# Quantised feed-forward constants set up by DMA and spread over two batches, with x's statistics first, in a fused cross-attention and feed-forward kernel

## The reference, cut to what matters

```
qh = softmax(Wq @ layernorm(x), over the 64 of a head) * 64**-0.5
kh = softmax(Wk @ c, over tokens);  vh = Wv @ c
out = Wo @ ((kh vh^T)^T qh) + bo
x = x + out / |out| * g * sqrt(128)            # |out| over the channels
w = (nibbles(qweight) - round(zeros / scales)) * scales      # 1024 x 1024
x = x + layernorm(x) @ w + bias
```

## Time and profile before

| | us |
|---|---|
| median of 3 runs (lowest, highest) | 718.89 (718.29, 720.46) |
| the profiled execution | 714.72 |
| its span | 712.7 |
| busy in the span: PE, DVE, POOL, ACT | 657.2, 547.1, 482.8, 448.7 |
| SyncE's 17 loads at the start, first issue to last issue's end | 0.74 to 9.14 |

### The profile page before, as it was taken

One profiled execution on the slowest core, in us unless ns is written; L12 is line 12 of the kernel. 1 busy time (PEld: TensorE's weight loads), 2 busy tenths in 40 slices (PEclk: granted clock), 3 DMA queues, 4 the chain that ended last, 5 costly groups with the idle time before them and its releaser, 6 DMA issues.

```text
span 712.7 us, 11165 instructions
## 1 busy us (share of the span) xinstructions
PE 657.2 (92%) x3328; PEld 420.9 (59%) x3328; DVE 547.1 (77%) x891; ACT 448.7 (63%) x744; POOL 482.8 (68%) x413
## 2 busy tenths in 40 slices
PE   4878699999999999999999999999999999999576
PEld 3645466666666666666666666666666666666242
DVE  3996897888888887888788887888788887886421
ACT  3676758567675847576675857576674857575402
POOL 3156484967769594967869494967859494967622
PEclk9979999999999999999999999999999999999888
DMA  8135235473625536373625536373635534353401
GB/s 295 60 59 126 52 68 139 94 174 89 159 53 160 102 82 153 88 177 81 161 52 152 108 82 158 89 177 72 166 57 161 95 85 101 88 118 90 102 17 59
DMA packets 178871, 78.43 MB, mean 110 GB/s; under 512 B 168328, under 2 KB 169888, under 8 KB 178848
## 3 DMA queue, kind: packets, MB, share of 16 engines
q1 hardware_dynamic: 172512, 55.09, 36.3%
q10 hardware_dynamic: 6336, 23.07, 9.5%
HBM read 28.32 MB, written 8.39 MB: 52 GB/s over the span
## 4 chain that ended last, share of the span: by engine, by line
PE 35%; POOL 25%; issue 19%; DVE 11%; ACT 6%; DMA 1%; SPq 1%; POOLq 0%; ACTq 0%; DVEq 0%
PE ps_m L1148 7%; POOL q_tok_lo L416 6%; PE ps_m L1080 4%; POOL x L489 3%; POOL q_exp L406 3%; POOL y L422 3%; DVE q_sum L809 3%; POOL c_lo L452 3%; PE ps_k L1010 3%; PE ps_k L1012 2%; PE ps_k L1011 2%; POOL rn L471 2%; ACT k_exp L537 2%; PE ps_o L1010 2%; DVE q_nmax L797 2%
## 5 line engine op out<-in xcount | busy, mean ns | idle before, releaser
L416 POOL TENSOR_TENSOR q_tok_lo<-q_exp,q_tok_hi 128x1024 f16<-128x1024 f32 x64 | 139.2, 2175 | 86.0 <-ACT q_tok_hi L553 85.9
L406 POOL TENSOR_TENSOR q_exp<-q_exp,q_rec 128x1024 f32<-128x1024 f32 x64 | 122.1, 1908 | 5.0
L1080 PE MATMUL ps_m<-k_t,c_t 128*128 128x512 f32 x256 | 120.0, 602 | 0.0
L790 DVE TENSOR_REDUCE k_nmax<-ps_k 128x1 f32<-128x1024 f32 x64 | 78.0, 1219 | 39.5 <-PE ps_k L1012 39.3
L542 ACT ACTIVATE q_exp<-q_exp 128x512 f32<-128x512 f32 x128 | 80.5, 629 | 44.2 <-DVE q_exp L802 44.1
L537 ACT ACTIVATE k_exp<-ps_k,k_nmax 128x1024 f32<-128x1024 f32 x64 | 71.0, 1110 | 53.8 <-DVE k_nmax L790 53.8
L553 ACT ACTIVATE q_tok_hi<-q_exp 128x1024 f16<-128x1024 f32 x64 | 67.6, 1056 | 54.4 <-POOL q_exp L406 54.4
L797 DVE TENSOR_REDUCE q_nmax<-ps_q 128x8 f32<-128x512 f32 x128 | 87.2, 681 | 11.2 <-PE ps_q L1012 9.6
L802 DVE TENSOR_TENSOR q_exp<-ps_q,q_nmax 128x512 f32<-128x512 f32 x128 | 88.5, 691 | 5.1 <-DVE q_nmax L797 0.2
L1010 PE MATMUL ps_q<-wq_hi,xn_lo 128*128 128x512 f32 x128 | 74.9, 585 | 7.2 <-DVE q_exp L802 5.7
L809 DVE TENSOR_REDUCE q_sum<-q_exp 128x16 f32<-128x1024 f32 x64 | 77.3, 1208 | 0.7 <-ACT q_exp L542 0.7
(11 more groups left out here) (162 smaller groups left out, 1384.8 us busy)
## 6 DMA issues: line engine op xcount, KB each, us to landing
x_res<-in_x ACTq DMA_DIRECT2D x16, 512.0 KB, 3.4
out_x<-y SPq DMA_DIRECT2D x15, 512.0 KB, 2.9
x_in<-in_x ACTq DMA_DIRECT2D x14, 512.0 KB, 4.5
c_in<-in_ctx ACTq DMA_DIRECT2D x14, 512.0 KB, 6.1
x_in<-in_x SPq DMA_DIRECT2D x2, 512.0 KB, 6.1
c_in<-in_ctx SPq DMA_DIRECT2D x2, 512.0 KB, 7.5
q_hi<-q_tok_hi SPq DMA_TRANSPOSE x64, 3.1
q_lo<-q_tok_lo SPq DMA_TRANSPOSE x64, 3.1
```

The lines of the kernel that those rows point to most:

```text
L406: nc.gpsimd.tensor_tensor(pair, pair, rec.unsqueeze(2).to_broadcast([P, 2 * HEADS, DH]), ALU.mult).then_inc(qs_done, 1)
L416: nc.gpsimd.tensor_tensor(q_tok_lo[p % 2][:], q_exp[:, 2 * p:2 * p + 2, :].rearrange("p t d -> p (t d)"), q_tok_hi[p % 2][:], ALU.subtract ...
L1080: last = nc.tensor.matmul(ps_m[:], c_t[s][:, t, :], k_t[:, t, :], start=(t == 0), stop=(t == TC - 1))
```

## The change

1. scale_bc is filled by one DMA that repeats the row of scales over 128 partitions. The zero and bias rows are split into three bf16 parts while they lie on 8 partitions (row_parts, 8x2x3x128) by ScalarE, GpSimd, ScalarE, GpSimd, and twelve small DMAs on SyncE's queue lay them into ffn_rows, which GpSimd has cleared first. The row transposes, their copies, the mixing and the wide splits are gone, as are zero_bc, bias_bc, cols and row_pick.
2. The nibbles of two weight tiles (both halves) are taken in iteration 0 at j = 1, 3, 5, 6 and those of the other two in iteration 1 at j = 1, 2, 3, 5; their second buffer is a tile of its own, so x_res is loaded without waiting for them. GpSimd's first write of x2 waits for all eight.
3. In iteration -1 x's statistics, `ve`, `rstd`, xn and xn_hi come ahead of c_abs's followers; GpSimd takes c_lo after `rstd`; `set_up_rows` moves here; TensorE projects k ahead of the second group of c transposes.
4. vo is copied by ScalarE instead of VectorE. gs_undo becomes a tensor_scalar with gs_col as its scalar, in every iteration.

```diff
@@ sync
             load_c(1, 1)
+            sp.dma_start(scale_bc[:], scales.rearrange("o a -> (a o)").partition_broadcast(P)).then_inc(scale_spread, 16)
+            sp.wait_ge(consts_made, 10)
+            for part in range(3):
+                sp.wait_ge(rows_split, (1, 3, 4)[part])
+                for r in range(4):
+                    row = 32 * part + r
+                    sp.dma_start(ffn_rows[row:row + 1, :].rearrange("a (t c) -> a t c", t=TC),
+                                 row_parts[:, r // 3, part, :]).then_inc(rows_placed, 16)
@@ gpsimd
+            nc.gpsimd.memset(ffn_rows[:], 0.0).then_inc(consts_made, 1)
...
+                first = isinstance(i, int) and i == FIRST
+                if first:
+                    fit_x()
+                    low_c()
...
+                if isinstance(i, int) and i == 0:
+                    both = rows_in[:, 1:3, :]
+                    pool.wait_ge(rows_split, 1)
+                    nc.gpsimd.tensor_tensor(both, both, row_parts[:, :, 0, :], ALU.subtract).then_inc(rows_split, 1)
+                    pool.wait_ge(rows_split, 3)
+                    nc.gpsimd.tensor_tensor(row_parts[:, :, 2, :], both, row_parts[:, :, 1, :],
+                                            ALU.subtract).then_inc(rows_split, 1)
...
+                                if isinstance(i, int) and i == 1:
+                                    pool.wait_ge(nibble_done, 2 * RC)
@@ scalar
-                if 1 <= j < 4:
-                    row = (scale_bc, zero_bc, bias_bc)[j - 1]
-                    for h in range(HALVES):
-                        act.wait_ge(rows_ready, 2 * (j - 1) + h + 1)
-                        nc.scalar.activation(halves(row)[h], ps_o[h][:], ACT.Copy).then_inc(rows_moved, 1)
...
+                    if j == 0 and isinstance(i, int) and i == 0:
+                        act.wait_ge(zero_steps, 5)
+                        nc.scalar.activation(row_parts[:, :, 0, :], rows_in[:, 1:3, :], ACT.Copy).then_inc(rows_split, 1)
...
+                    if isinstance(i, int) and i == 0 and j == 0:
+                        move_vo()
                         act.wait_ge(rows_split, 2)
+                        nc.scalar.activation(row_parts[:, :, 1, :], rows_in[:, 1:3, :], ACT.Copy).then_inc(rows_split, 1)
+                    if isinstance(i, int) and i == 0 and j in (2, 4, 6, 7):
+                        convert_nibble((2, 4, 6, 7).index(j))
...
+                    if isinstance(i, int) and i == 1 and j in (2, 3, 4, 6):
+                        convert_nibble(4 + (2, 3, 4, 6).index(j))
@@ vector
+            def pick_nibble(k):
+
+                m, high = NIBBLES[k]
                 if k == 0:
...
                     dve.wait_ge(qw_loaded, 16 * RC)
                 elif k > 1:
                     dve.wait_ge(w_converted, k - 1)
...
-                nc.vector.tensor_scalar(q_nibble[k % 2], q_packed[k % RC], 4 * (k // RC), 15, ALU.logical_shift_right,
+                nc.vector.tensor_scalar(q_nibble[k % 2], q_packed[m], 4 * high, 15, ALU.logical_shift_right,
                                         ALU.bitwise_and).then_inc(nibble_done, 1)
...
-                    nc.vector.tensor_tensor(gs_undo[:], g_undo[:], gs_col[:], ALU.mult).then_inc(fit_steps, 1)
+                    if isinstance(i, int) and i == 0:
+                        dve.wait_ge(gs_done, 1)
+                    nc.vector.tensor_scalar(gs_undo[:], g_undo[:], gs_col[:], None, ALU.mult).then_inc(fit_steps, 1)
...
+                if isinstance(i, int) and i == FIRST:
+                    stats_x()
+                    mean_x()
+                    abs_c()
+                    norm_x()
+                    set_up()
                     set_up_rows()
+                    top_c()
+                    max_k(n, 0)
+                    return
@@ tensor
-            def set_up_row(k):
...
-                    last = nc.tensor.transpose(ps_o[k % 2][:, t * P:(t + 1) * P], col.to_broadcast([P, P]),
-                                               ident[:])
-                last.then_inc(rows_ready, 1)
...
+                    if j == 7 and do_n and isinstance(i, int) and i == FIRST:
+                        project_k(n, 0)
                     if j == 7 and do_n:
                         transpose_c(1)
```

More of the change, by code:

```diff
@@ L89, in build @@
         scale_bc = sb("scale_bc", [P, OUT])
-        zero_bc = sb("zero_bc", [P, OUT])
-        bias_bc = sb("bias_bc", [P, OUT])
+        nibble = sb("nibble", [P, OUT])
         bo_col = sb("bo_col", [P, 1])
@@ L288, in loads @@
             return 8 * (b - s) + 16
+        NIBBLES = [(m + 2 * late, high) for late in range(2) for high in range(2) for m in range(2)]
         FIRST, LAST = -1, NB + 2
@@ L449, in iteration @@
                         low_q(a, 0)
-                    if j == 3 and do_n:
-                        pool.wait_ge(chi_done, n + 1)
-                        nc.gpsimd.tensor_tensor(c_lo[:], c_in[1 - s][:], c_hi[:].bitcast(F32),
-                                                ALU.subtract).then_inc(clo_done, 1)
+                    if j == 3 and do_n and not first:
+                        low_c()
                     if j == 4 and do_a:
@@ L461, in iteration @@
                         add_y(f, 1)
-                    if j == 6 and do_n:
-                        pool.wait_ge(stats1_done, n + 1)
-                        nc.gpsimd.tensor_tensor(ve1[:], mv1[:, 1:2], eps_col[:], ALU.add).then_inc(ve1_done, 1)
-                        pool.wait_ge(ve1_done, n + 1)
-                        nc.gpsimd.tensor_tensor(rstd1[:], ve1[:], neg_half[:, 0:1], ALU.pow).then_inc(rstd1_done, 1)
+                    if j == 6 and do_n and not first:
+                        fit_x()
                     if j == 6 and do_c:
@@ L538, in exp_k, with high_x @@
                                          accum_out=k_sum[:, sums, j:j + 1]).then_inc(kexp_done, 1)
+                first = isinstance(i, int) and i == FIRST
+                def high_x():
+                    act.wait_ge(xn_done, n + 1)
+                    if begun(8 * a):
+                        act.wait_ge(q_ready, 8 * a)
+                    nc.scalar.activation(xn_hi[1 - s][:], xn[:], ACT.Copy).then_inc(xnhi_done, 1)
                 def exp_q(j):
@@ L1256, in iteration @@
                         mix_m(4, 5)
-                    if j == 7 and do_n:
+                    if j == 7 and do_n and not (isinstance(i, int) and i == FIRST):
                         project_k(n, 0)
```

196 lines of the change are left out of this document (79 added, 117 removed).

## The result

| | before | after |
|---|---|---|
| median (lowest, highest), 6 runs each, us | 718.68 (717.06, 720.46) | 707.78 (705.42, 709.09) |
| the profiled execution; its span | 714.72; 712.7 | 707.34; 705.5 |

The ratio is 0.9854, 95% interval 0.9834 to 0.9874: faster by 1.46%, some 10.5 us.

A forecast was written before the change was run, and what follows sets the result against it. The prediction took VectorE as the engine to relieve in batch 0. Savings up to the end of batch 0 (-6.2), batch 1 (-1.3) and +0.5 given back made -7.0 us: 711.9 us from a median of 718.89, range 708.3 to 716.5.

The forecast's parts named there:

- A: Prologue: first k projection ahead of the second c transposes, c_t copy on ScalarE, rows_in transposes gone; -0.8 us.
- B: ScalarE in batch 0: the two zero_bc copies leave the chain ahead of the k_t copy; -0.97 us.
- C: Batch 0 to the third q_sum: nibble and gs_undo relieved on VectorE, GpSimd and ScalarE then limit; another -3.4 us.
- D: End of batch 0: an exponential no longer waits for the k maximum that stood behind nibble 7; -1.0 us.
- E: Batch 1: VectorE's mixing of 2.0 us gives way to one nibble of 0.7; -1.3 us.
- F: Batch 1, given back: two of its four nibbles fall on a GpSimd operation; +0.5 us, bounds 0 and 2.3.
- Clock: Less TensorE work in batches 0 and 1 brings half rate: no change, 717.9 us (0.11), or slower, 722 (0.05).
- Port collisions: VectorE's nibble picks hold up other GpSimd operations, six times 0.45 us: 2.7 us lost, 714.6; chance 0.14.
- More than said: The shorter gs_undo also gains 0.3 us in each of the fourteen later batches: 4.2 us more, 707.7; chance 0.08.

The follow-up runs named there:

- before_again: The kernel before, unchanged, executed again for a second profile: 717.32 us.
- gs_only: The kernel before with only gs_undo changed to its new tensor_scalar form: ratio 0.9996 to the kernel before.
- before_fill_gaps: The kernel before with 29 unread transposes added on TensorE in three gaps of batch 1: ratio 0.9997 to the kernel before.
- rows_only: The kernel before with only the scale, zero and bias rows split on 8 partitions and placed by DMA: 713.0 us, ratio 0.9940 to the kernel before.
- nibbles_batch0: The changed kernel with all eight nibbles in batch 0 and none in batch 1: ratio 0.9897 to the kernel before.
- old_first: The changed kernel with the whole first iteration in its old order: ratio 0.9888 to the kernel before.
- no_gs: The changed kernel with gs_undo in its old two-tensor form: ratio 0.9843 to the kernel before.
- after_fourth: The changed kernel, unchanged, executed once more as a yardstick: 707.79 us, ratio 0.9862 to the kernel before.
- mix_back: rows_only with the cost of the old mixing, two VectorE operations, put back into batch 1: 715.28 us, ratio 0.9965 to the kernel before.
- split_back: rows_only with the old splitting of the rows put back into batch 1 on scratch tensors: 716.43 us, ratio 0.9974 to the kernel before.
- fill_batch0: The changed kernel with forty unread transposes added on TensorE in batch 0: ratio 0.9900 to the kernel before.

## Why the prediction was wrong

The direction and the places were right, the size too small. By its steps, with the mean of the marks over the four profiles of the changed kernel and over four of the old order with the row work (before, before_again, gs_only, before_fill_gaps):

| stretch | predicted | measured |
|---|---|---|
| up to K (A) | -0.8 | 17.30 to 16.87: -0.4, within the scatter of K |
| K to q_tok_hi (rest of A, B) | -1.0 | 20.78 to 18.84: -1.9 |
| q_tok_hi to m_t, batch 0 (C, D) | -4.4 | 24.25 to 19.83: -4.4 |
| batch 1 (E, F) | -0.8 | 43.77 to 40.20: -3.6 |
| behind it | 0 | 609.4 to 610.5: +1.1, over code that didn't change (scatter 3 us) |

The four first lines make -10.4 us, with the fifth it is -9.3; the runs have 9.6 to 10.5.

**The step that failed is E**, batch 1, together with the execution that it was worked out on: "VectorE's mixing ... (0.74 + 1.28 = 2.0 us) ... One nibble of 0.7 takes their place: -1.3", and "Splitting bias_bc and ffn_rows on VectorE (1.22 twice) is replaced by two nibbles". I priced the row work of batch 1 by the length of its instructions and traded it one for one against nibbles. E and F together had -0.8; over four profiles each, batch 1 went from 43.77 to 40.20 us, -3.6, and the longest batch 1 of the changed kernel (40.52) is shorter than the shortest of the old (41.60). Two things were left out. The first is the queue behind a split: ScalarE's two copies of 32 rows ("paid back by the four w_int") hold an exponential of q, and VectorE's subtraction waits for them. The second is TensorE's rate. TensorE's wait for k_t was 1.55 us in rows_only and nibbles_batch0, with a clock of 1.00 and 0.95 over the batch, 2.70 in the changed kernel (0.92), 2.91 and 2.51 with a part put back (0.92 and 0.84) and 3.85 before (0.81 to 0.92). How far the rate falls differs between executions of nearly the same program: before, before_again and gs_only, which has only the form of gs_undo changed and the same time, take 41.60, 43.79 and 45.92 us for batch 1 at a granted clock of 0.92, 0.84 and 0.81, all with a wait of 3.85.

How large the miss is for the row work alone isn't settled. By its one profile it is worth 7.5 us in batch 1 (36.27 against 43.77), and the four nibbles that come back cost 3.9. By the runs the whole row part is worth 4.3 us where the terms had 3.3, and that difference is within the noise.

**Second, the base.** "I take the saving from the profiled execution and apply it to the median." The 4.2 us between the two were not spread evenly: 2.2 of them are batch 1's (41.60 against a mean of 43.77), just the stretch that the change shortens and makes steady (39.44 to 40.52). So of the 2.8 us by which batch 1 was missed, 2.2 are this step's; against the profiled execution alone batch 1 gained 1.4 where E and F had 0.8. The prediction gave 707.7 for the profiled execution, and the changed kernel's median is 707.78: the 4.2 us that were added on top were no longer there.

**A**: "its projection stands behind the transposes and gains about as much; I add nothing". The first query waited for xn_lo (1.42 us before, 1.47 in old_first), not for the transposes; old_first's profile puts that at 1.5 us, its runs at 1.6 to 2.4 within the noise told above. Also "2 us of cover are left" for the row arithmetic was too much. VectorE's timeline after:

```profile
11.55 1.35 DVE L755 TENSOR_TENSOR rows_in<-rows_in,inv_scale 8x128 f32<-8x128 f32 x1
12.94 2.28 DVE L757 TENSOR_SCALAR rows_in<-rows_in 8x128 f32<-8x128 f32 x1
...
15.60 0.21 DVE L762 CAST ident<-ident 128x128 bf16<-128x128 f32 x1
15.73 0.27 DVE L869 TENSOR_REDUCE c_top<-ps_o 128x1 f32<-128x128 f32 x1
```

GpSimd's c_lo and xn_lo ran then, and two operations on 8 partitions took 1.35 and 2.28 instead of 0.28 and 0.2 us. The arithmetic ends at 15.8, right at the maximum (15.93), and not at 13.7; the loads had landed in time.

**C and D** held: the nibbles are gone, GpSimd and ScalarE decide then, and the stretch has the predicted length. **B**'s 0.97 us is shown by no run: with the row copies gone and nothing else, the stretch up to q_tok_hi got no shorter (rows_only 22.17), and what the changed kernel gained there can be the order's. In C the 2.13 us of gs_undo were rightly not added on top (the limit by GpSimd took them).

**F**: two nibbles met GpSimd, 1.84 and 2.53 us, that is 3.0 above 0.7 each; bounded at 2.3, taken at 0.5. What that costs isn't shown: the last nibble took 0.63 us in no_gs and 2.12 in after_fourth, and their batches 1 took 39.59 and 39.44.

**The rivals.** "Clock" was right that the rate moves and wrong on what it costs. In the second half of batch 0 the clock did fall, from 0.82 to 0.86 down to 0.71 to 0.75, and the stretch was still 4.4 us shorter, since other engines decide there. In batch 1 slow stretches come behind waits on other engines, and the change makes TensorE's wait for k_t shorter. The Trainium skill (TensorE: Matmul & The Clock Gate, "What's actually happening") says that activity releases the throttle. By that, work that fills a wait can be worth more than it costs, and the trace agrees in batch 1 of the changed kernel (29 transposes more, 2.6 us less); in the kernel before the same 29 gave nothing. "Port collisions" was seen (the nibbles, the row arithmetic), smaller than the gains. "More than said" is refuted by gs_only and no_gs.

**What stays open.** How batch 1 before divides between the queue and the clock wasn't separated: filling the gap there failed to hold the rate. More profiles of rows_only, mix_back and split_back would tell whether the lengths of batch 1 or the runs are right. From the three executions of the old batch 1, 10.8 us more at half rate (2 x (0.19 x 45.92 - 0.08 x 41.60)) go with 4.3 us more of batch, 0.4 per us; at that, its first execution would be some 39 us at full rate, against 36.27 of rows_only. That is an estimate from two executions. Why K moves by 2.6 us was not looked into either.

## What to carry to other kernels

Work on one engine's queue costs what stands behind it, not its own length (gs_undo's 2.13 us on the chain were worth nothing): list that for each removed and each added instruction, short ones too. Before a sum is made on one profiled execution, set it against the median; where they are apart, look for the stretch that changes from one execution to the next, since it is the one that an edit can make steady. The same holds for the experiments: a stretch in one profile is not the price of a part until the runs bear it out, and here they gave less than half. Where TensorE waits and its next matmuls are at half rate, filling the wait with matmuls that nobody reads is a cheap test of what the rate costs; here it was a gain in the changed kernel and none in the one before. The fillers must wait for nothing themselves.

## What the runs showed of the hardware

- The mean granted clock of one stretch differs between executions of the same instructions by 0.08 (batch 1 before: 0.92 and 0.84), with 2.2 us of length.
- One element per partition is enough for a collision: gs_undo as tensor_tensor took 0.16 to 2.13 us in rows_only (median 1.13), as tensor_scalar with a scalar by address 0.213 to 0.215 in all sixteen batches. The Trainium skill (SBUF — State Buffer, "Who interferes with whom") has the two-input operation contend with GpSimd's reads, and the trace agrees; it also says that tensor_scalar can contend, and the trace has that for wide and for short ones (a nibble 2.53, an 8x128 one 2.28 us), not for the 128x1 ones read here.
- A ScalarE copy of 32x1024 takes 1.06 us, the one of 128x1024 1.04 to 1.06.
- In the second half of batch 0 a clock of 1.00 (fill_batch0) and one of 0.74 give the same 19.5 us (at 0.71 to 0.73 it is 20.5 to 20.7): there the lower rate of 0.74 cost nothing, as other engines decide.
